# A decoder layer of self attention, cross attention and a quantised feed-forward on one core: orders rewritten step by step, grouped loads and stores, half of one mask moved from TensorE to VectorE

## The chip, the cores and the metric

The kernel runs on one core of a Trainium2 chip. The metric is device time in microseconds (us) of one execution, from the first to the last instruction of the program. Lower is better. The inputs are in the device's memory (HBM) before the time starts. How the host lays them out beforehand is not in the time.

## The reference

For each of B = 32 batches of S = 128 rows and D = 128 columns, three residual blocks follow one another, each on a layer-normalised x.

```python
x = x + self_attn(layernorm(x))        # 16 heads of 8, relative sinusoidal bias, no mask
x = x + cross_attn(layernorm(x), ctx)  # 16 heads of 8, keys and values from ctx, mask of padded keys
x = x + ffn(layernorm(x))              # w_down(silu(gate) * up), 128 -> 512 -> 128,
                                       # weights ternary, activations rounded to 8 bits
# attention: softmax(q @ k.T * scale + bias), masked scores set to -1e9, then @ v, then @ w_out
# ffn input and hidden rows: x * 127 / max|x|, rounded, each with its own scale
```

The batches are independent. Within a batch everything is a chain.

## The kernel before, in words

**Pipeline over batches.** One step of the program handles many batches, each at another stage. In the names S is self attention, X cross attention, F the feed-forward, and a lag is how many steps behind the newest batch a stage is: projections of S at lag 0, its scores for the maxima (scores A) at 2, its scores for the exponentials (scores B) and attention at 3, the same for X at 4, 5 and 6, its output and the first feed-forward half at 7, the second half at 8. So in a full step all engines work on nine batches. Steps 0 to 9 and 30 to 39 are written out. The twenty between are a loop on each engine with four steps in its body, and addresses and waited counts come from registers there.

**Order.** The five queues (TensorE = PE, VectorE = DVE, ScalarE = ACT, GpSimd = POOL, and SyncE = SP, which issues all DMAs) each run a fixed list of operations per step, `step(st)`, written by hand. Semaphores alone tie them together.

**Attention.** q and k are split into three bf16 parts each (`qk_parts`), written to a scratch in HBM (`parts_out`) and read back (`stack_in`) into `stack_q` and `stack_k`, so that one bf16 matmul with 72 (X) or 120 (S) rows gives a score to float32 accuracy. The 16 heads go in four chunks c = 0..3 of four heads, 512 columns, one bank. Scores A (L1059) go to `bank_a[c % 2]`; DVE takes the negative row maxima (`row_max`, L826), POOL splits them in two bf16 parts, PE transposes them (L1154, 32 columns), ACT copies them out, and SP stores them as two more rows of `stack_q` (`max_in`, L327). Scores B (L1092) then come out transposed and with the maximum subtracted in `bank_b[c % 2]`, and ACT takes the exponential (L533) into `probs`, which S and X share. `attend` (L1117) multiplies a chunk by the values in four column tiles of 32.

**Mask.** X alone has one. POOL makes `mask_bias` (0 or -1e30, bf16), and PE adds it to each chunk of scores A and scores B by one matmul of 512 columns with the identity:

```python
masked = a == "X"
if masked:
    pe.matmul(bank[:, :], ident_bf[:], mask_bias[:, p, :].unsqueeze(1).to_broadcast([S, HC, S]),
              start=True, stop=False)
```

**The rest.** `ctx` is loaded batch by batch (L337), transposed by PE (L1178) and copied by ACT (`ctxT_out`). The mask is loaded batch by batch (L347) and the result stored batch by batch (L356). x is loaded in three pieces, the last of 24 batches (1.5 MB) at step 2. `keep_warm` (L1026) puts four idle matmuls ahead of scores B of the first four batches. `normalise("S")` (L743) writes `xn_S`, `normalise("X")` `xn_X`; `residual` is L855; `o_transposed` is L1138; `h_gate` L894. POOL's `rest` is L432, `part3` L440.

## Time and profile before

| | |
|---|---|
| Median of 3 runs | 514.36 us (513.71 to 518.05) |
| Profiled execution, first to last instruction | 513.4 us |
| PE busy | 454.1 us, 88% |
| DVE busy | 398.0 us, 78% |
| ACT busy | 372.9 us, 73% |
| POOL busy | 254.6 us, 50% |
| DMA | 62.48 MB, mean 122 GB/s |
| Chain that ended last | PE 78% of the span |

The profiled execution took 513.4 us by its span, which is its own time too; no other time of it is given. Busy time of an engine is the union of its instructions; the weight loads of PE are counted apart. The shares are means over three stretches: a start of about 100 us in which the pipeline fills, some 300 us of full steps, and an end in which it empties. The term "turn" below means the time from one full step to the next.

### The profile page before, as it was taken

The numbers are of one execution on the slowest core, as the hardware profiler recorded it, in microseconds if no ns is written. First come the engines' busy times: TensorE is split into PE (matmuls) and PEld (weight loads), VectorE is DVE, ScalarE is ACT, GpSimd is POOL, SyncE is SP. The second block draws the span as 40 slices with busy tenths as digits, with TensorE's granted clock in tenths as the row PEclk, the third lists the DMA queues.
The fourth block names the chain that finished last, engine by engine and source line by source line (L and its number), as shares of the span: only waits on it lengthen the run. The fifth ranks groups of instructions, "written<-read, shape, count | busy, mean of one in ns | idle before, by whom it ended". The sixth has DMA issues, their size and how long they took to land.

```text
span 513.4 us, 18365 instructions
## 1 busy us (share of the span) xinstructions
PE 454.1 (88%) x5596; PEld 328.0 (64%) x5596; DVE 398.0 (78%) x1154; ACT 372.9 (73%) x993; POOL 254.6 (50%) x691
## 2 busy tenths in 40 slices
PE   2246889999999999999999999999999999997762
PEld 1224556777777777777777777777777777764440
DVE  5722446799888889888888988889888888877553
ACT  0222556788888888888888888888888887775451
POOL 4221445655565555555566655555556654434110
PEclk9999789999999999999999999999999999999785
DMA  6264255555455545454445555544454555223000
GB/s 186 77 192 107 72 143 142 140 142 141 134 134 144 141 122 145 139 135 131 122 138 135 135 128 135 137 135 122 133 137 137 137 137 136 79 86 92 23 7 10
DMA packets 82191, 62.48 MB, mean 122 GB/s; under 512 B 57634, under 2 KB 71714, under 8 KB 82146
## 3 DMA queue, kind: packets, MB, share of 16 engines
q1 hardware_dynamic: 82146, 61.92, 44.4%
q8 instruction: 23, 0.38, 0.3%
q14 instruction: 22, 0.18, 0.1%
HBM read 46.47 MB, written 14.88 MB: 119 GB/s over the span
## 4 chain that ended last, share of the span: by engine, by line
PE 78%; DVE 5%; DMA 4%; issue 4%; SPq 3%; ACT 3%; POOL 1%; DVEq 0%; POOLq 0%; ACTq 0%
PE bank L1117 14%; PE bank L1092 12%; PE bank L1059 11%; PE bank L1088 6%; PE bank L1055 6%; PE bank L1264 4%; PE bank L1210 3%; PE bank L1138 2%; PE bank L1237 2%; PE bank L1175 2%; PE bank L1154 2%; PE bank L1295 2%; PE bank L1303 2%; PE bank L1224 2%; PE bank L1196 2%
## 5 line engine op out<-in xcount | busy, mean ns | idle before, releaser
L533 ACT ACTIVATE probs<-bank 128x512 f32<-128x512 f32 x256 | 145.5, 597 | 32.0 <-PE bank L1092 31.7
L826 DVE TENSOR_REDUCE neg_max_S<-bank 128x4 f32<-128x512 f32 x128 | 87.1, 685 | 34.3 <-PE bank L1059 34.2
L826 DVE TENSOR_REDUCE neg_max_X<-bank 128x4 f32<-128x512 f32 x128 | 84.2, 676 | 8.9 <-PE bank L1059 5.7
L1059 PE MATMUL bank<-stack_k_S,stack_q_S 120*128 120x128 bf16 x512 | 46.9, 227 | 12.9 <-DMA stack_k_S<-scratch_S 12.4
L432 POOL TENSOR_TENSOR qk_rest_X<-qk_X,qk_parts_X 128x256 f32<-128x256 f32 x32 | 21.4, 670 | 70.8 <-ACT qk_parts_X L536 70.8
L1092 PE MATMUL bank<-stack_q_S,stack_k_S 122*128 122x128 bf16 x512 | 52.5, 229 | 4.5 <-DMA stack_q_S<-neg_maxT_S 4.5
L1117 PE MATMUL bank<-probs,v_aug_S 128*32 128x128 f32 x1024 | 55.5, 291 | 0.0
L1055 PE MATMUL bank<-mask_bias,ident_bf 128*128 128x512 bf16 x128 | 49.4, 386 | 3.6 <-issue 2.3
L1092 PEld LDWEIGHTS bank<-stack_q_X,stack_k_X 74*128 74x128 bf16 x512 | 40.6, 99 | 16.4 <-issue 1.6
L1092 PE MATMUL bank<-stack_q_X,stack_k_X 74*128 74x128 bf16 x512 | 50.8, 222 | 0.0
L1088 PE MATMUL bank<-ident_bf,mask_bias 128*128 128x512 bf16 x128 | 50.3, 393 | 0.0
L1059 PE MATMUL bank<-stack_k_X,stack_q_X 72*128 72x128 bf16 x512 | 50.1, 220 | 0.0
L1059 PEld LDWEIGHTS bank<-stack_k_X,stack_q_X 72*128 72x128 bf16 x512 | 39.9, 98 | 16.0 <-issue 0.6
L1059 PEld LDWEIGHTS bank<-stack_k_S,stack_q_S 120*128 120x128 bf16 x512 | 36.8, 101 | 15.3 <-issue 14.0
L1092 PEld LDWEIGHTS bank<-stack_q_S,stack_k_S 122*128 122x128 bf16 x512 | 32.4, 101 | 21.2 <-issue 7.8
L855 DVE TENSOR_TENSOR x_all<-bank,x_all 128x128 f32 (+1 forms) x64 | 18.6, 291 | 25.7 <-PE bank L1264 24.3
L536 ACT ACTIVATE o_raw<-bank 128x256 f32<-128x256 f32 x64 | 24.8, 388 | 16.7 <-PE bank L1117 16.7
L1117 PE MATMUL bank<-probs,v_aug_X 128*32 128x128 f32 x1024 | 34.6, 276 | 0.0
L440 POOL TENSOR_TENSOR qk_parts_S<-qk_rest_S,qk_parts_S 128x256 bf16<-128x256 f32 x32 | 21.6, 675 | 21.0 <-ACT qk_parts_S L536 21.0
L609 ACT ACTIVATE hT<-bank,minus_round 128x512 bf16<-128x512 f16 x32 | 22.0, 686 | 12.4 <-PE bank L1295 12.4
L1117 PEld LDWEIGHTS bank<-probs,v_aug_S 128*32 128x32 f32 x1024 | 20.6, 109 | 14.8 <-issue 1.2
L1117 PEld LDWEIGHTS bank<-probs,v_aug_X 128*32 128x32 f32 x1024 | 26.0, 109 | 4.8 <-ACT probs L533 1.3
(159 smaller groups left out, 1159.1 us busy)
## 6 DMA issues: line engine op xcount, KB each, us to landing
stack_q_S<-scratch_S SPq DMA_DIRECT2D x32, 288.0 KB
stack_k_S<-scratch_S SPq DMA_DIRECT2D x96, 96.0 KB
stack_q_X<-scratch_X SPq DMA_DIRECT2D x32, 288.0 KB
stack_k_X<-scratch_X SPq DMA_DIRECT2D x96, 96.0 KB
scratch_S<-qk_parts_S SPq DMA_DIRECT2D x32, 192.0 KB, 2.3
scratch_X<-qk_parts_X SPq DMA_DIRECT2D x32, 192.0 KB, 2.3
ctx_in<-ctx SPq DMA_DIRECT2D x32, 64.0 KB, 2.7
mask_in<-mask SPq DMA_DIRECT2D x32, 64.0 KB, 1.8
```

The lines of the kernel that those rows point to most:

```text
L432: pool.tensor_tensor(qk_rest[a][:], qk[a][:], qk_parts[a][:, :, 0, :], ALU.subtract)\
L440: pool.tensor_tensor(qk_parts[a][:, :, 2, :], qk_rest[a][:], qk_parts[a][:, :, 1, :], ALU.subtract).then_inc(sems["part3_" + a], 1)
L533: act.activation(probs[:, c, :], bank_b[c % 2][:, :], ACT.Exp).then_inc(sems["exp_" + a], 1)
L536: return act.activation(out_ap, in_ap, ACT.Copy)
L609: act.activation(hT[:].rearrange("p c s -> p (c s)"), bank_t[:, 0:256].bitcast(F16), ACT.Identity, bias=minus_round16[:, 0:1]).then_inc(se ...
L826: dve.tensor_reduce(neg_max[a][:, first_head(c):first_head(c) + 2 * HC - 1:2], bank_a[c % 2][:, :].rearrange("i (h j) -> i h j", h=HC), AX ...
L1055: pe.matmul(bank[:, :], ident_bf[:], mask_bias[:, p, :].unsqueeze(1).to_broadcast([S, HC, S]), start=True, stop=False)
L1059: last = pe.matmul(bank[:, part_of_bank(hh)], stack_q[a][rows, p, head(c, hh)], stack_k[a][rows, p, head(c, hh)], start=not masked, stop=n ...
L1088: pe.matmul(bank[:, :], mask_bias[:, p, :], ident_bf[:].unsqueeze(1).to_broadcast([S, HC, S]), start=True, stop=False)
L1092: last = pe.matmul(bank[:, part_of_bank(hh)], stack_k[a][rows, p, head(c, hh)], stack_q[a][rows, p, head(c, hh)], start=not masked, stop=n ...
L1117: last = pe.matmul(bank_o[32 * hh:32 * hh + 32, half * S:(half + 1) * S], v, probs[:, c, part_of_bank(hh)], start=u == 0, stop=u == 1, ski ...
L1264: pe.matmul(quarter(bank_s, 2), oT[a][:], w_o[a][:], start=True, stop=True)\
```

## The change

It keeps the pipeline of batches and all arithmetic except where said, and does the following.

- **Steps.** All 42 steps are written out; there is no loop and no register. Each operation takes the step and its own lag. Lags differ per engine by one where its list starts at another place of the step. On PE the operations are told which operations used their bank before (`*users`), and `after` waits for the first of these that exists.
- **Orders.** All five lists are new. On PE the four `attend("S")` stand together, as do the four of X.
- **Mask.** `BIASED = (0, 2)`: in chunks 0 and 2 of X's scores A, PE adds no mask. `row_max` on DVE adds it and takes the maximum head by head with `tensor_tensor_reduce`, instead of one `tensor_reduce` of four heads. Scores B keep the mask on PE.
- **Context.** The host hands `ctx` over transposed. PE's transpose and ACT's copy of it are gone. It and the mask are loaded for four batches at once (`group_load`), the results of the first 28 batches stored by four.
- **Buffers.** `probs` and `o_raw` are one each for S and X, values have four copies, the transposed `xn_X` goes to `bank_o`, and `neg_max_parts` is 128 wide with zeros, so that its transpose uses all 128 columns.
- q, k and v of a batch are projected together (`project_qkv`).

```diff
+STEPS = [(t, t) for t in range(-1, B + 9)]
+GROUP, GROUP_LAG = 4, 2
+BIASED = (0, 2)
...
-        probs = sb("probs", [S, CH, HC * S])
-        o_raw = sb("o_raw", [128, 2, S])
+        probs = {a: sb(f"probs_{a}", [S, CH, HC * S]) for a in "SX"}
+        o_raw = {a: sb(f"o_raw_{a}", [128, 2, S]) for a in "SX"}
+        biased = sb("biased", [S, CH, HC, S], BF16)
...
+            def group_load(st):
+
+                n = st.of("X", GROUP_LAG)
+                if n is None or n % GROUP:
+                    return
+                batches = slice(n, n + GROUP)
+                sp.dma_start(ctxT[:, batches, :], ctx[batches].rearrange("b d s -> d b s"))\
+                    .then_inc(sems[f"ctx_loaded{n // GROUP % 2}"], 16)
+                sp.dma_start(mask_in[:, batches, :], mask[batches].rearrange("b s t -> s b t"))\
+                    .then_inc(sems[f"mask_loaded{n // GROUP % 2}"], 16)
...
             def step(st):
-                if st.base == 2:
+                if st.of("S", 2) == 0:
                     load_x(2)
-                max_in("X", st.seq(B_X))
-                ctx_load(st.seq(CTX_T - 1))
-                stack_in("S", st.seq(FRONT_S + 1))
-                store(st.seq(FFN2))
-                parts_out("X", st.seq(FRONT_X))
-                max_in("S", st.seq(A_S))
-                mask_load(st.seq(A_X - 1))
-                parts_out("S", st.seq(FRONT_S))
-                stack_in("X", st.seq(FRONT_X))
...
+                group_load(st)
+                parts_out("S", st, 0)
+                stack_in("X", st, 4)
+                max_in("X", st, 5)
+                stack_in("S", st, 0)
+                parts_out("X", st, 3)
+                store(st, 7)
+                max_in("S", st, 1)
...
+                if a == "X" and c in BIASED:
+                    if c == BIASED[0]:
+                        dve.wait_ge(sems["mask_bias"], done(b))
+                        if b:
+                            dve.wait_ge(sems["max_X"], done(b - 1, CH))
+                    for hh in range(HC):
+                        head = first_head(c) + 2 * hh
+                        last = dve.tensor_tensor_reduce(biased[:, c, hh, :], quarter(bank_a[c % 2], hh), mask_bias[:, b % 2, :],
+                                                        -1.0, -2.0 * BIG, ALU.add, ALU.min,
+                                                        neg_max[a][:, head:head + 1])
+                    last.then_inc(sems["max_" + a], 1)
+                    return
...
+                masked = a == "X" and c not in BIASED
```

**PE, the part of a full step that holds the attention of S.** Before, with one `attend` of four matmuls at a time (`v_aug_S`), L1237 the transpose of X's output, L1224 and L1225 X's projections, L1264 its output projection:

```order
L1117 MATMUL bank<-probs,v_aug_S 32x128 x4
L1092 MATMUL bank<-stack_q_S,stack_k_S 128x128 x4
L1117 MATMUL bank<-probs,v_aug_S 32x128 x4
L1237 MATMUL bank<-ident,o_norm_X 128x128
L1224 MATMUL bank<-xnT_X,w_cross_sb 128x128
L1225 MATMUL bank<-ctxT,w_cross_sb 128x128
L1117 MATMUL bank<-probs,v_aug_S 32x128 x4
L1264 MATMUL bank<-w_out_x_sb,oT_X 128x128
L1036 REGISTER_ALU
L1059 MATMUL bank<-stack_k_S,stack_q_S 128x128 x4
L1117 MATMUL bank<-probs,v_aug_S 32x128 x4
```

And the same part after the change, where L1049 is scores B, L1029 scores A, L1065 `attend`, L1110 to L1112 the three projections, L1138 the output projection:

```order
L1049 MATMUL bank<-stack_q_S,stack_k_S 128x128 x4
L1110 MATMUL bank<-xnT_X,w_cross_sb 128x128
L1111 MATMUL bank<-ctxT,w_cross_sb 128x128
L1112 MATMUL bank<-w_cross_sb,ctxT 128x128
L1138 MATMUL bank<-w_out_x_sb,oT_X 128x128
L1029 MATMUL bank<-stack_k_S,stack_q_S 128x128 x4
L1065 MATMUL bank<-probs_S,v_aug_S 32x128 x16
L1161 MATMUL bank<-ident_h,h_q 128x128 x4
```

The four attentions of S, which stood apart between work on the whole array, are one block of sixteen.

**DVE, around the maxima of X, chunks 1 to 3.** Before:

```order
L743 TENSOR_SCALAR xn_S<-x_all,mv_S,rstd_S 128x128
L886 TENSOR_SCALAR y_q<-xn_F,y_inv 128x128
L822 REGISTER_ALU
L826 TENSOR_REDUCE neg_max_X<-bank 128x4
L822 REGISTER_ALU
```

```order
L797 TENSOR_REDUCE neg_max_X<-bank 128x4
L862 TENSOR_SCALAR y_q<-xn_F,y_inv 128x128
L703 TENSOR_SCALAR xn_S<-x_all,mv_S,rstd_S 128x128
L792 ISA biased,neg_max_X<-bank,mask_bias 128x128
L792 ISA neg_max_X 128x1
```

The normalisation of S has moved behind the rounding of y and the maxima of chunk 1, and the pair of L792 rows stands four times in a row for chunk 2 and four times for chunk 0, eight pairs in a step for two reductions.

**SP, from the second batch's scratch at the start of the program.** Before, with the third piece of x, one context, the stacks of batch 1 and the maxima of batch 0:

```order
L288 DMA scratch_S<-qk_parts_S 128x6x128
L233 DMA x_all<-x 128x24x128
L337 DMA ctx_in<-ctx 128x128
L306 DMA stack_q_S<-scratch_S 72x1x2048
L311 DMA stack_k_S<-scratch_S 24x1x2048 x3
L327 DMA stack_q_S<-neg_maxT_S 2x16x128
```

After:

```order
L271 DMA scratch_S<-qk_parts_S 128x6x128
L283 DMA stack_q_S<-scratch_S 72x1x2048
L288 DMA stack_k_S<-scratch_S 24x1x2048 x3
L300 DMA stack_q_S<-neg_maxT_S 2x16x128
L222 DMA x_all<-x 128x24x128
L309 DMA ctxT<-ctx 128x4x128
L311 DMA mask_in<-mask 128x4x128
L271 DMA scratch_S<-qk_parts_S 128x6x128
L283 DMA stack_q_S<-scratch_S 72x1x2048
L288 DMA stack_k_S<-scratch_S 24x1x2048 x3
L300 DMA stack_q_S<-neg_maxT_S 2x16x128
```

The large load of x has moved behind the stacks of batch 1 and the maxima of batch 0, now together with four contexts and masks, and ahead of the scratch, stacks and maxima of the next batch.

## Rows read from the trace of the kernel before

**Rows 1.** The page's chain of work that ended last, by engine.

```profile
PE 78%; DVE 5%; DMA 4%; issue 4%; SPq 3%; ACT 3%; POOL 1%; DVEq 0%; POOLq 0%; ACTq 0%
```

**Rows 2.** A window of full steps: length, busy us (instructions) per engine, PEclk, DMA, GB/s.

```profile
200.00:300.00 100.00, 99.47 (x1299) 73.39 (x1296) 88.52 (x261) 86.49 (x233) 57.43 (x155) 1.00 0.49 134
```

**Rows 3.** Timeline of ACT, one instruction per step: start us, duration us.

```profile
103.27 0.71 ACT L656 ACTIVATE tanh_g<-bank,gate_half 128x512 f32<-128x512 f32 x1
116.30 0.71 ACT L656 ACTIVATE tanh_g<-bank,gate_half 128x512 f32<-128x512 f32 x1
...
249.86 0.71 ACT L656 ACTIVATE tanh_g<-bank,gate_half 128x512 f32<-128x512 f32 x1
...
356.94 0.71 ACT L656 ACTIVATE tanh_g<-bank,gate_half 128x512 f32<-128x512 f32 x1
...
409.81 0.71 ACT L656 ACTIVATE tanh_g<-bank,gate_half 128x512 f32<-128x512 f32 x1
```

**Rows 4.** The chain in order of time, one full step: start us, us, what.

```profile
250.04 1.01 PE bank L1117 x32
251.05 0.33 PE bank L1092 x4
251.53 0.33 PE bank L1092 x4
251.87 0.22 PE bank L1138 x2
...
252.54 0.23 PE bank L1092 x4
...
253.30 0.36 PE bank L1117 x8
...
257.27 0.22 PE bank L1055
...
263.29 1.01 PE bank L1117 x32
```

**Rows 5.** Timeline of DVE in a full step; in brackets idle before, and for whom.

```profile
276.69 0.29 DVE L855 TENSOR_TENSOR x_all<-bank,x_all 128x128 f32 x1
276.90 0.28 DVE L724 BATCH_NORM_STATS2 stats_S<-x_all 128x6 f32 x1
...
281.17 0.14 DVE L938 TENSOR_TENSOR h_scale<-h_inv,h_unit 128x1 f32<-128x1 f32 x1
281.24 0.68 DVE L826 TENSOR_REDUCE neg_max_S<-bank 128x4 f32<-128x512 f32 x1
282.37 0.29 DVE L855 TENSOR_TENSOR x_all<-bank,x_all 128x128 f32 x1 [0.45 <-PE bank L1264]
282.59 0.69 DVE L826 TENSOR_REDUCE neg_max_S<-bank 128x4 f32<-128x512 f32 x1
283.20 0.28 DVE L724 BATCH_NORM_STATS2 stats_F<-x_all 128x6 f32 x1
...
286.84 0.79 DVE L743 TENSOR_SCALAR xn_S<-x_all,mv_S,rstd_S 128x128 f32 x1
```

**Rows 6.** Timeline of POOL at the same time.

```profile
286.87 0.67 POOL L432 TENSOR_TENSOR qk_rest_S<-qk_S,qk_parts_S 128x256 f32<-128x256 f32 x1 [0.24 <-ACT qk_parts_S L536]
```

**Rows 7.** Groups by line and shape: busy us, mean ns, idle before.

```profile
L826 DVE TENSOR_REDUCE neg_max_X<-bank 128x4 f32<-128x512 f32 x128 | 84.2, 676 | 8.9 <-PE bank L1059 5.7
L743 DVE TENSOR_SCALAR xn_S<-x_all,mv_S,rstd_S 128x128 f32 x20 | 15.4, 772 | 0.0
L536 ACT ACTIVATE ctxT<-bank 128x128 f32<-128x128 f32 x32 | 8.8, 276 | 0.0
L743 DVE TENSOR_SCALAR xn_X<-x_all,mv_X,rstd_X 128x128 f32 x20 | 6.9, 346 | 3.1 <-POOL rstd_X L416 2.3
```

**Rows 8.** Timeline of SP's DMA issues at the start of the program.

```profile
29.45 0.90 SPq L233 DMA_DIRECT2D x_all<-x  x1
30.40 5.66 SPq L337 DMA_DIRECT2D ctx_in<-ctx  x1
...
39.22 0.70 SPq L327 DMA_DIRECT2D stack_q_S<-neg_maxT_S  x1
```

**Rows 9.** Timeline of PE, first scores B of batch 0.

```profile
42.73 1.03 PE L1092 MATMUL bank<-stack_q_S,stack_k_S 122*128 122x128 bf16 x8 [4.50 <-DMA stack_q_S<-neg_maxT_S]
```

More of the change, by code:

```diff
@@ L211, in first_head, with done, loaded, in_group @@
             return H // 2 * (c // 2) + c % 2
[L213 to L225 removed]
+        def done(b, per=1, upto=None):
+            return b * per + (per if upto is None else upto)
+        def loaded(b, per):
+            return (b // 2 + 1) * per
+        def in_group(b):
+            return (b // GROUP // 2 + 1) * 16
+        def after(eng, st, *users):
+            for name, lag, *signal in users:
+                stage = name[-1] if name[-2:] in ("_S", "_X") else "F"
+                b = st.of(stage, lag)
+                if b is not None:
+                    eng.wait_ge(sems[name], done(b, CH, signal[0]) if signal else done(b))
+                    return
+        def run(step):
+            for s, x in STEPS:
+                step(Step(s, x))
         block = es.enter_context(nc.Block())
@@ L995, in _ @@
+                ln_moments("S", st, -1)
+                gated(st, 8)
+                attend_sums("X", st, 7)
+                normalise("X", st, 4)
+                attend_norm("X", st, 7)
+                h_max(st, 8)
+            run(step)
         @block.tensor
@@ new lines, in scores_a @@
+                if masked:
+                    pe.wait_ge(sems["mask_bias"], done(b))
+                    pe.matmul(bank[:, :], ident_bf[:], mask_bias[:, b % 2, :].unsqueeze(1).to_broadcast([S, HC, S]),
+                              start=True, stop=False)
+                for hh in range(HC):
+                    last = pe.matmul(bank[:, part_of_bank(hh)], stack_q[a][rows, b % 2, head(c, hh)],
+                                     stack_k[a][rows, b % 2, head(c, hh)], start=not masked,
+                                     stop=not masked or hh == HC - 1)
@@ new lines, in scores_a, with scores_b @@
+                last.then_inc(sems["score_a_" + a], 1)
+            def scores_b(a, st, lag, c, *users):
+                b = st.of(a, lag)
+                if b is None:
+                    return
+                bank, rows = bank_b[c % 2], slice(0, A_ROWS[a] + M_ROWS)
+                after(pe, st, *users)
+                if c == 0 and a == "S" and b < WARM_BATCHES:
+                    keep_warm(bank)
+                if c == 0:
+                    pe.wait_ge(sems[f"max_in_{a}{b % 2}"], loaded(b, 16))
@@ L1094, in scores_b, with attend @@
+                    last = pe.matmul(bank[:, part_of_bank(hh)], stack_k[a][rows, b % 2, head(c, hh)],
+                                     stack_q[a][rows, b % 2, head(c, hh)], start=not masked,
                                      stop=not masked or hh == HC - 1)
                 last.then_inc(sems["score_b_" + a], 1)
-            def attend(a, st, b, c):
-                if not b:
+            def attend(a, st, lag, c, *users):
+                b = st.of(a, lag)
+                if b is None:
```

1233 lines of the change are left out of this document (543 added, 690 removed).

## The prediction

> **What bounds the kernel now.** I read first the chain that ended last: PE holds 78% of it and nothing else more than 5% [rows 1]. Then the window of full steps: in 100 us PE is busy 99.5, DVE 88.5, ACT 86.5, POOL 57.4, at full clock and half-used DMA engines [rows 2]. So in full steps PE is the bound and two engines run close behind it; the reader should see that 11 us of each 100 is all that a cheaper PE can win before DVE is the bound. Third, one instruction per step on ACT gives the turn. From 103.27 to 409.81 us lie 23 turns, 13.33 us each; the first of them, outside the loop, took 13.03, eight in the loop took 107.08, 13.39 each [rows 3]. So 23 full turns are 306.5 of the 513.4 us; the start takes 103 and the end another 103. The profiled span, 513.4, lies 1.0 below the median of 514.36; I work on the span and add 1.0 at the end.
>
> **PE, part by part.** In the chain one full step runs from 250.04 to 263.29 [rows 4].
>
> - Loop: written out, a turn is 13.03 instead of 13.33 on average: -0.30. The price of it, more instructions to fetch, shows nowhere in the written-out steps of before.
> - Two mask matmuls of 512 columns go, 0.22 each on the chain [rows 4]: -0.44.
> - The context's transpose: two transposes of 128 columns took 0.22 (L1138) [rows 4], one is 0.11: -0.11. ACT loses a copy of 0.28 [rows 7].
> - The attentions of S: apart, four matmuls (counted as 8) cost 0.36, so four times 1.44; X's sixteen in a block cost 1.01 [rows 4]. In a block: -0.43.
> - What follows a matmul that uses 32 columns costs more: scores B took 0.33 behind the attention of X and behind the transposed maxima (251.05 and 251.53) and 0.23 elsewhere (252.54) [rows 4]. Three places behind S's attentions and two behind the transposed maxima go, at 0.10 each: -0.5, between 0.2 and 0.9 as the gap of 0.15 ahead of 251.53 is also theirs or is not.
>
> Sum: 13.33 - 1.8 = 11.55 us per turn of PE work (11.2 to 11.9). If PE stayed the bound, that would be 41 us off 23 turns.
>
> **DVE, part by part.** Its busy time is 88.5% of 13.33 = 11.8 us per turn [rows 2].
>
> - Out: two reductions of 512 columns, 0.68 each [rows 7]: -1.35.
> - In: eight times an addition with maximum over 128 columns, with the accumulator read behind it (two instructions by the build), which the trace of before does not show. I bound a pair from both sides. What counts is the distance between starts, not the duration: the addition of the same shape with one operand in a bank lasts 0.29 but the next one starts 0.21 later; the reduction lasts 0.69 and its follower starts 0.61 later; an instruction of one column lasts 0.14 and its follower starts 0.07 later [rows 5]. So 0.28 a pair at the low end. At the high end nothing overlaps, since the read needs the finished sum: 0.29 + 0.15 = 0.44. I take 0.31, near the low end, as all three rows show the overlap: +2.5 (2.25 to 3.5).
> - `xn_S` lasts 772 ns in the loop, the same operation of X 346 [rows 7]; it runs from 286.84 to 287.63, beside POOL's subtraction from 286.87 to 287.54, and ends just after it [rows 5, 6]. In the new order it stands elsewhere; whether it meets POOL again I cannot see: between -0.43 and 0, I take -0.2.
> - The register instructions go; they are not in the busy time.
>
> Sum: 11.8 - 1.35 + 2.5 - 0.2 = 12.75 us (12.3 to 13.9). That is more than PE's 11.55: **DVE becomes the bound**, and of PE's 1.8 us most has nowhere to go. DVE now waits 0.45 us for X's output projection (L1264) and elsewhere in each turn [rows 5]; with PE 1.2 us ahead of it such waits should nearly vanish. I leave 0.05. A turn of **12.8 us**.
>
> [...]
>
> **ACT and POOL.** ACT's 86.5% is 11.5 us, less the copy of 0.28: 11.25, still below. POOL has 7.7 of 13.3. The chain around a step from S's projection over ACT, POOL, ACT (parts, values) to `gate_up`, `tanh` and `gate` has little slack in the new order. It is covered as long as DVE has its row maxima to do; were that cover gone, I would expect a wait of some 0.3 us at `h_gate`.
>
> **SP and the DMAs.** The maxima of X are stored after `stack_in("X")` as before. PE now wants them nearer to their transpose: between L1088 of X and the first scores B of X stand about 3.8 us of PE work by the prices of rows 4, before about 6 (from 251.5 to 257.5) [rows 4]. The path of copy, issue and landing took 3.5 us at the start, where one was issued at 39.22 and its reader began at 42.73 [rows 8, 9]. That is close, but PE has 1.2 us to spare. Grouped loads and stores save SP issues only, and SP is nowhere in the chain of full steps: 0.
>
> **Start.** Before, the load of 24 batches of x went out at 29.45, the next issue behind it took 5.66 us, and the maxima of batch 0, issued at 39.22, reached PE at 42.73 [rows 8, 9]. Now these maxima and the stacks of batch 1 go first, and I expect those scores 3 us earlier. But then x with four contexts and masks, a third more bytes (2.0 MB), stands ahead of the scratch, stacks and maxima of the next batch, which PE wants 12 us later. The gain is given back there: 0, plus or minus 3.
>
> **The sum.** 23 full turns: 23 x (12.8 - 13.33) = -12.2. Start and end have about nine turns with attention but no feed-forward or no new batch, in which DVE has less to do and PE's saving counts in part; I take 0.5 each, -4.5 (0 to -9). The last turns, pure latency of one batch, stay. 513.4 - 12.2 - 4.5 = 496.7, and with 1.0 for the median **497.5 us**. With the turn between 12.5 and 13.0 it is 490 to 503.
>
> **The rivals.**
>
> - *PE stays the bound or the pair is cheap (0.25), and `xn_S` is free of POOL.* DVE is then at 12.05, PE at 11.55, the turn about 12.2: -26, and -6 outside: 482. For it: the overlap in rows 5. Against it: no row has an accumulator read.
> - *Waits take half the gain.* DVE is the bound and PE must wait for it in every bank pair; PE's fixed order then makes ACT or DVE idle for 0.4 us in each turn, at `h_gate` or at the maxima of X that come late. Turn 13.2: -3, and -3 outside: 508. For it: 0.45 us and more of such waits now, and three engines above 11 us.
> - *Slower: the accumulator read waits for its instruction's end.* One mechanism on DVE at L792: 8 x 0.44 = 3.5, the turn 13.85, +12 over 23 turns, -4 outside: 522. It decides from a pair of 0.37 on, where DVE reaches 13.25, the turn of today.
> - *The change does not do what it says:* PE's cheaper step is not seen as the 32-column switches stay, and DVE and PE both end near 13.2: the loop's 0.3 is cancelled, 512.
>
> **How the numbers follow.** Forecast 0.50, cheap pair 0.13, waits 0.17, slower 0.13, no effect 0.07. Less than 1%, 5 us, cannot be told from no change in this kernel. Faster by over 1% (under 509): 0.50 + 0.13 and two thirds of the waits, 0.75. Slower by over 1% (over 519.5): 0.10. Same: 0.15. For the range I leave out part of the cheap case and the slower one: 483 to 514.
>
> **What would show it.** In the profile after, DVE should be busy 95% or more in full steps and PE near 90%; the chain should name DVE lines, L792 first, instead of 78% PE. Sixteen attentions of S should take 1.0 us. The eight pairs should take 2.5 us from first to last start of their blocks; at 3.5 the forecast is wrong and the kernel slower. `xn_S` should be near 350 or near 770 ns. The first scores B should start near 40 us and the start as a whole should be no shorter. Wrong would make it: a price of the pair far from 0.31, waits of DVE for PE or ACT of more than 0.5 us per turn, or straight-line code that makes an engine wait for its instructions.

## The result, and the profile after

The changed kernel took 505.03 us (median of 4 runs, 497.83 to 509.43), the kernel before in the same session 516.20 (4 runs, 513.71 to 520.06): ratio 0.9685, 95% interval 0.960 to 0.977, faster. The ratio is taken over the fast executions alone, which are 497.83 and 502.48 of the changed kernel (median 500.2) and all four of before; by the two medians it would be 0.978. The forecast was 497.5 in a range of 483 to 514. The profiled execution is the fastest of the four: 497.83 us, span 496.0, against 513.4 before.

The page after has these lines on the engines and on the chain.

```profile
PE 412.5 (83%) x5500; PEld 316.3 (64%) x5500; DVE 402.9 (81%) x1602; ACT 364.7 (74%) x961; POOL 251.3 (51%) x693
issue 30%; POOL 24%; DMA 14%; PE 13%; SPq 8%; DVE 5%; ACT 4%; POOLq 0%; ACTq 0%; DVEq 0%
DMA stack_k_X<-scratch_X 7%; SPq L288 3%; POOL qk_rest_X L400 3%; POOL mask_bias L437 3%; POOL qk_rest_S L400 3%; POOL qk_parts_X L409 3%; DMA scratch_S<-qk_parts_S 2%; PE bank L1029 2%; POOL x_all L390 2%; PE bank L1049 2%; DMA scratch_X<-
```

Of the 78% of [rows 1] PE keeps 13% of the chain. DVE, which the forecast named, has 5%. POOL has 24%, in many lines of at most 3%, and 30% is time in which an engine waited for nothing that the profile shows. What heads the lines that can be named is a transfer, the load of X's stacks. The windows say why: the first is the one of [rows 2], the other two are two neighbouring turns.

```profile
200.00:300.00 100.00, 96.01 (x1368) 75.62 (x1356) 95.05 (x392) 89.39 (x241) 60.81 (x168) 1.00 0.54 145
233.26:245.53 12.27, 12.02 (x175) 9.48 (x179) 11.92 (x50) 11.17 (x30) 7.58 (x22) 1.00 0.48 133
245.53:258.64 13.11, 12.14 (x175) 9.53 (x178) 11.84 (x50) 11.36 (x30) 7.91 (x22) 1.00 0.66 184
```

PE and DVE are each busy 95% or more. In the second turn PE is busy 0.12 us more than in the first and DVE 0.08 less; it is 0.84 us longer because both wait. ACT's one instruction per step gives all turns, as in [rows 3].

```profile
105.00 0.69 ACT L613 ACTIVATE tanh_g<-bank,gate_half 128x512 f32<-128x512 f32 x1
...
245.53 0.69 ACT L613 ACTIVATE tanh_g<-bank,gate_half 128x512 f32<-128x512 f32 x1
258.64 0.69 ACT L613 ACTIVATE tanh_g<-bank,gate_half 128x512 f32<-128x512 f32 x1
...
395.39 0.69 ACT L613 ACTIVATE tanh_g<-bank,gate_half 128x512 f32<-128x512 f32 x1
```

There are two kinds of turn: a **quiet turn** of 12.27 us, and between such ones a **long turn** of 13.0 to 13.8; of the 23 turns from 105.00 to 395.39, seven are long. The mean is 290.39 / 23 = 12.63. PE's timeline in the long turn above answers to [rows 4].

```profile
250.15 1.08 PE L1065 MATMUL bank<-probs_S,v_aug_S 128*32 128x128 f32 x32
251.20 0.40 PE L1161 MATMUL bank<-ident_h,h_q 128*128 128x128 f16 x4
...
252.75 0.38 PE L1029 MATMUL bank<-stack_k_X,stack_q_X 72*128 72x128 bf16 x4 [0.81 <-DMA stack_k_X<-scratch_X]
```

S's sixteen attentions now stand in one block, 1.05 us from start to next start. PE then stands still for X's stack, 0.81 us. DVE at the same time, as in [rows 5]:

```profile
253.17 0.29 DVE L792 CUSTOM_DVE_ANT_0 biased<-bank,mask_bias 128x128 bf16<-128x128 f32 x1 [0.59 <-PE bank L1029]
253.38 0.08 DVE L792 DVE_READ_ACCUMULATOR2_ANT neg_max_X<- 128x1 f32 x1
253.38 0.29 DVE L792 CUSTOM_DVE_ANT_0 biased<-bank,mask_bias 128x128 bf16<-128x128 f32 x1
253.59 0.08 DVE L792 DVE_READ_ACCUMULATOR2_ANT neg_max_X<- 128x1 f32 x1
...
256.38 0.49 DVE L862 TENSOR_SCALAR y_q<-xn_F,y_inv 128x128 f16<-128x128 f32 x1
256.80 0.33 DVE L703 TENSOR_SCALAR xn_S<-x_all,mv_S,rstd_S 128x128 f32<-128x128 f32 x1
```

From one pair to the next is 0.21 us, and the accumulator read starts together with the next addition (both at 253.38): it adds nothing to the 0.21 us from the addition of `residual` at 276.69 to its follower [rows 5]. Over the program the two L792 groups below have 256 records each, 32 batches by eight heads, so one `tensor_tensor_reduce` stands in the trace as an addition and a read. Within a block of four, additions start 0.20 to 0.22 us apart, 192 times, and each time the read has the start of the next addition. In this turn `xn_S` is free of POOL, and `y_q` has its place beside POOL's addition, which ran from 256.34 to 256.80. In the quiet turn before it both meet POOL, with 0.51 us for `y_q` and 0.49 for `xn_S`; in the kernel before they took 0.289 and 0.772 in the mean. The groups over the whole program, as in [rows 7]:

```profile
L792 DVE CUSTOM_DVE_ANT_0 biased<-bank,mask_bias 128x128 bf16<-128x128 f32 x256 | 58.6, 283 | 13.4 <-PE bank L1029 13.3
L792 DVE DVE_READ_ACCUMULATOR2_ANT neg_max_X<- 128x1 f32 x256 | 20.6, 81 | 0.0
L862 DVE TENSOR_SCALAR y_q<-xn_F,y_inv 128x128 f16<-128x128 f32 x32 | 14.1, 440 | 0.1
L703 DVE TENSOR_SCALAR xn_S<-x_all,mv_S,rstd_S 128x128 f32<-128x128 f32 x32 | 14.0, 437 | 5.9 <-POOL rstd_S L383 5.9
```

The quiet turn has a chain over three engines that the trace of before did not show as a wait: `y_q` on DVE, its transpose on PE, the copy `yT` on ACT, S's output projection on PE (L1138), and the residual on DVE.

```profile
243.16 0.51 DVE L862 TENSOR_SCALAR y_q<-xn_F,y_inv 128x128 f16<-128x128 f32 x1
243.73 0.23 PE L1130 MATMUL bank<-ident_h,y_q 128*128 128x128 f16 x1
244.10 0.36 ACT L584 ACTIVATE yT<-bank,minus_round 128x128 bf16<-128x128 f16 x1
244.60 0.46 PE L1138 MATMUL bank<-w_out_s_sb,oT_S 128*128 128x128 f32 x2 [0.17 <-ACT yT L584]
245.10 0.29 DVE L827 TENSOR_TENSOR x_all<-bank,x_all 128x128 f32<-128x128 f32 x1 [0.17 <-PE bank L1138]
```

From 105 to 402 us PE waits for `yT` 16 times, 2.8 us in all, and DVE for that projection 23 times, 4.4 us; PE's waits of the kernel before, from 103 to 410 us, have no such line.

SP's issues and PE at the start answer to [rows 8, 9].

```profile
38.03 0.70 SPq L300 DMA_DIRECT2D stack_q_S<-neg_maxT_S  x1
39.28 0.85 SPq L222 DMA_DIRECT2D x_all<-x  x1
```

```profile
40.06 0.62 PE L1049 MATMUL bank<-stack_q_S,stack_k_S 122*128 122x128 bf16 x8 [2.01 <-DMA stack_q_S<-neg_maxT_S]
...
57.83 1.03 PE L1049 MATMUL bank<-stack_q_S,stack_k_S 122*128 122x128 bf16 x8 [2.47 <-DMA stack_q_S<-neg_maxT_S]
```

The first scores B start at 40.06 instead of 42.73; those of the next batch, at 57.83, came at 55.44 before.

Where the stack waits come from is seen in SP's issues around that turn, before in the first fence and after in the second, which begins with a quiet turn's.

```profile
277.12 2.01 SPq L311 DMA_DIRECT2D stack_k_X<-scratch_X  x3
```

```profile
233.84 2.03 SPq L288 DMA_DIRECT2D stack_k_X<-scratch_X  x3
...
244.16 0.41 SPq L309 DMA_DIRECT2D ctxT<-ctx  x1
244.63 0.50 SPq L311 DMA_DIRECT2D mask_in<-mask  x1
245.23 0.45 SPq L271 DMA_DIRECT2D scratch_S<-qk_parts_S  x1
...
246.62 2.03 SPq L288 DMA_DIRECT2D stack_k_X<-scratch_X  x3
```

Before, the last of X's stacks was issued by 279.1 and its scores A began at 283.78: 4.7 us. After, it is issued by 248.65, and PE would have begun at 251.94: 3.3 us, and in this turn 0.5 MB of contexts and masks stand ahead of it in the queue. In the quiet turn the last is issued by 235.87 and its scores A begin at 239.51 without a wait: 3.6 us are just enough there. In the long turn the stack is there 4.1 us after its issue. PE waits for X's stack six times from 105 to 402 us, 6.6 us in all, and the seventh long turn has 0.7 us at the same place, where the view names a maximum of DVE. Two of the six (1.20 us at 124.87, 1.45 at 176.94) have no grouped load ahead of them; why those stacks came late is not traced.

### The profile page after: what moved, and what is told of

It reads as the page before. It is cut to its first block, busy times and chain, and to the rows that moved or that the text cites. A ratio compares the mean times of both kernels' runs of the same rounds, so it can differ in the third digit from the quotient of the medians.

```text
span 496.0 us, 17508 instructions
## 1 busy us (share of the span) xinstructions
PE 412.5 (83%) x5500; PEld 316.3 (64%) x5500; DVE 402.9 (81%) x1602; ACT 364.7 (74%) x961; POOL 251.3 (51%) x693
## 4 chain that ended last, share of the span: by engine, by line
issue 30%; POOL 24%; DMA 14%; PE 13%; SPq 8%; DVE 5%; ACT 4%; POOLq 0%; ACTq 0%; DVEq 0%
DMA stack_k_X<-scratch_X 7%; SPq L288 3%; POOL qk_rest_X L400 3%; POOL mask_bias L437 3%; POOL qk_rest_S L400 3%; POOL qk_parts_X L409 3%; DMA scratch_S<-qk_parts_S 2%; PE bank L1029 2%; POOL x_all L390 2%; PE bank L1049 2%; DMA scratch_X<-qk_parts_X 2%; POOL rstd_F L383 2%; POOL rstd_S L383 2%; SPq L283 2%; PE bank L1110 1%
## 5 line engine op out<-in xcount | busy, mean ns | idle before, releaser
L506 ACT ACTIVATE probs_S<-bank 128x512 f32<-128x512 f32 x128 | 73.0, 599 | 10.0 <-PE bank L1049 10.0
L506 ACT ACTIVATE probs_X<-bank 128x512 f32<-128x512 f32 x128 | 72.4, 595 | 10.4 <-PE bank L1049 10.4
L792 DVE CUSTOM_DVE_ANT_0 biased<-bank,mask_bias 128x128 bf16<-128x128 f32 x256 | 58.6, 283 | 13.4 <-PE bank L1029 13.3
L1029 PE MATMUL bank<-stack_k_X,stack_q_X 72*128 72x128 bf16 x512 | 50.0, 220 | 12.6 <-DMA stack_k_X<-scratch_X 9.6
L1029 PE MATMUL bank<-stack_k_S,stack_q_S 120*128 120x128 bf16 x512 | 46.1, 224 | 10.7 <-DMA stack_k_S<-scratch_S 10.2
L1029 PEld LDWEIGHTS bank<-stack_k_X,stack_q_X 72*128 72x128 bf16 x512 | 37.5, 98 | 23.7 <-DVE neg_max_S L797 11.1
L1049 PEld LDWEIGHTS bank<-stack_q_X,stack_k_X 74*128 74x128 bf16 x512 | 40.6, 99 | 16.2 <-issue 1.6
L1049 PE MATMUL bank<-stack_q_X,stack_k_X 74*128 74x128 bf16 x512 | 50.7, 222 | 0.0
L1049 PE MATMUL bank<-stack_q_S,stack_k_S 122*128 122x128 bf16 x512 | 45.8, 224 | 4.8 <-DMA stack_q_S<-neg_maxT_S 4.8
L1029 PEld LDWEIGHTS bank<-stack_k_S,stack_q_S 120*128 120x128 bf16 x512 | 36.1, 100 | 13.0 <-issue 10.6
L797 DVE TENSOR_REDUCE neg_max_X<-bank 128x4 f32<-128x512 f32 x64 | 43.3, 677 | 0.0
L1049 PEld LDWEIGHTS bank<-stack_q_S,stack_k_S 122*128 122x128 bf16 x512 | 34.5, 101 | 13.5 <-DMA stack_q_S<-neg_maxT_S 6.7
L1065 PE MATMUL bank<-probs_S,v_aug_S 128*32 128x128 f32 x1024 | 35.4, 280 | 0.0
L1065 PE MATMUL bank<-probs_X,v_aug_X 128*32 128x128 f32 x1024 | 34.6, 276 | 0.0
L1065 PEld LDWEIGHTS bank<-probs_X,v_aug_X 128*32 128x32 f32 x1024 | 26.0, 109 | 13.3 <-ACT probs_X L506 13.1
L400 POOL TENSOR_TENSOR qk_rest_S<-qk_S,qk_parts_S 128x256 f32<-128x256 f32 x32 | 21.4, 668 | 24.7 <-ACT qk_parts_S L509 24.6
L827 DVE TENSOR_TENSOR x_all<-bank,x_all 128x128 f32<-128x128 f32 x64 | 18.7, 291 | 17.6 <-PE bank L1138 16.8
L623 ACT ACTIVATE h_q<-h,round,h_scale 128x512 f16<-128x512 f32 x32 | 26.1, 814 | 5.0 <-DVE h_scale L924 5.0
```

The costliest lines, as they stand in the source:

```text
L400: pool.tensor_tensor(qk_rest[a][:], qk[a][:], qk_parts[a][:, :, 0, :], ALU.subtract)\
L506: act.activation(probs[a][:, c, :], bank_b[c % 2][:, :], ACT.Exp).then_inc(sems["exp_" + a], 1)
L623: act.activation(h_q[:], h[:], ACT.Identity, bias=round16[:, 0:1], scale=h_scale[:, 0:1])\
L792: last = dve.tensor_tensor_reduce(biased[:, c, hh, :], quarter(bank_a[c % 2], hh), mask_bias[:, b % 2, :], -1.0, -2.0 * BIG, ALU.add, ALU.min,
L797: dve.tensor_reduce(neg_max[a][:, first_head(c):first_head(c) + 2 * HC - 1:2], bank_a[c % 2][:, :].rearrange("i (h j) -> i h j", h=HC), AX ...
L827: dve.tensor_tensor(x_all[:, b, :], quarter(bank_s, 2), x_all[:, b, :], ALU.add)\
```

## The experiments

Each is the changed kernel with one edit, unless it says the kernel before. Ratios are to the kernel before, run between them on the same chip.

### Loads one batch at a time

```diff
-GROUP, GROUP_LAG = 4, 2
+GROUP, GROUP_LAG = 1, 2
```

> The changed kernel with contexts and masks loaded and results stored batch by batch (GROUP = 1 instead of 4), all else as in the change. In the changed kernel three turns of four last 12.26 us and the fourth 12.9 to 13.5; in the fourth, scores A of X wait for the stacks of X to land. Theory 1 (the burst of eight contexts and masks stands ahead of the stacks in the DMA queues): all turns become about 12.3, the DMA waits at scores A of X vanish in full steps, and the time falls by 5 to 9 us against the changed kernel (497.8 to 509.4), to 490 to 500. Theory 2 (the fourth turn is long for another reason, for instance the stored results or fetching of instructions): the pattern of four stays with GROUP = 1, or every turn grows by a little, and the time stays within 3 us.

Measured: 507.77 us, ratio 0.983 (0.975 to 0.991). The quiet turn stays 12.27, but eleven of 23 turns are long and the mean is 13.01 against 12.63. PE's waits from 105 to 402 us:

```profile
PE bank L1029 <- DMA stack_k_X<-scratch_X: 12.9, 13, 2.2
```

In the changed kernel that line reads 6.6 us, 6 times, 1.5 at most. So the pattern of four is gone, and neither theory holds as written: with a small load ahead of the stack in every turn, the waits for it come more often. Grouping moves these loads out of three of four turns, from in front of a stack that has little margin. I had put it at 0. The two profiled executions differ by 0.4 us a turn, but what grouping is worth in the time is not shown: 3.1 of the 8.8 us between the 23 turns are two falls of the clock (below), the profile here is of the slowest of four executions and the changed kernel's of the fastest, and the intervals of the two ratios overlap.

### All masks on PE, and all on DVE

```diff
-BIASED = (0, 2)
+BIASED = ()            # second kernel: (0, 1, 2, 3)
```

> The changed kernel with the whole mask on PE (BIASED empty): four pairs of reductions per turn come back as on the kernel before, in the new order. Theory 1 (VectorE is the bound at 12.27 us, the pairs cost 8 x 0.21 = 1.7 us there, two reductions 1.2 us, and PE has some 0.5 us or more to spare): a quiet turn of 11.8 to 12.1 us, the kernel 4 to 10 us faster than the changed one. Theory 2 (the moved mask is what makes the change fast, since PE is still as good as the bound): turn 12.7, 10 to 12 us slower than the changed one.

> The changed kernel with the whole mask of X's scores A on VectorE (BIASED = all four chunks). Theory 1 (VectorE is the bound): 16 pairs at 0.21 = 3.4 us instead of 1.7 + 1.2, so +0.5 us per turn, a quiet turn of 12.8 us and 12 to 15 us more than the changed kernel. Theory 2 (PE as good as the bound): turn 11.9 to 12.3, the same or 5 to 9 us faster.

Measured: all on PE 502.75, ratio 0.975 (0.967 to 0.983); all on DVE 504.20, ratio 0.981 (0.972 to 0.991). Both intervals overlap that of the changed kernel (0.960 to 0.977); the quiet turns tell them apart. The first row is a quiet turn with all masks on PE, the second with all on DVE.

```profile
284.38:296.77 12.39, 12.14 (x176) 9.70 (x181) 11.27 (x36) 11.35 (x30) 7.56 (x22) 1.00 0.51 134
```

```profile
230.39:242.91 12.52, 11.69 (x172) 9.28 (x175) 12.18 (x66) 11.19 (x31) 7.60 (x22) 1.00 0.47 131
```

With no pair on DVE the turn is 12.39 and PE's; with sixteen it is 12.52 and DVE's; with eight it is 12.27. Both theories of either run missed: each named one engine as the bound, and the turn grew in both directions. A mask matmul costs 0.22 us [rows 4], a reduction 0.61 [rows 5] and a pair 0.21 from start to start. If the end turns were all work, the changed kernel would have 12.39 - 2 x 0.22 = 11.95 us of it on PE and 12.52 - 8 x 0.21 + 2 x 0.61 = 12.06 on DVE. These are upper bounds, since both engines also wait in these turns; from the busy times, 12.14 and 12.18, the same sums give 11.70 and 11.72. The turn of 12.27 lies above all of them. **Of the three splits tried, two of four has the shortest quiet turn, and the whole move of the masks is worth 0.12 us a turn**, about 3 us of the time, which the medians can't show. PE's 0.44 has nowhere to go, as DVE is as full.

### The last load of x two steps later

```diff
-                if st.of("S", 2) == 0:
+                if st.of("S", 4) == 0:
                     load_x(2)
```

> The changed kernel with the third piece of x (24 batches, 1.5 MB) loaded at step 4 instead of step 2; the groups of contexts and masks stay at step 2. Theory 1 (that load stands ahead of the scratch, stacks and maxima of batches 1 and 2 and costs the start 5 to 8 us): the second batch's scores B begin near 51 to 53 us instead of 57.8 and the first tanh comes 3 to 6 us before 105.0; a wait of the same kind may appear later in the start and take back a part. Theory 2 (the start is bound by the chain of one batch per step, not by the load): the first tanh stays within 1 us of 105.

Measured: 499.96, ratio 0.972 (0.963 to 0.980), first tanh at 103.33 instead of 105.00, quiet turn 12.28, seven long turns in 23 as in the changed kernel. The second batch's scores B start at 50.05 instead of 57.83, so that load was in their way as theory 1 says, but 1.7 us is left of it at the first tanh, between the two theories. In the time it is nothing that can be told from the changed kernel.

### The kernel before, written out

```diff
-LOOP_FROM, LOOP_TO = 10, 30
+LOOP_FROM, LOOP_TO = 10, 10
```

> The kernel before with all 40 steps written out and no loop, nothing else. Theory 1 (the loop costs 0.3 us per turn, as the turns of before outside the loop last 13.03 to 13.2 and those inside 13.39): all full turns about 13.0 to 13.2, 4 to 7 us faster than before. Theory 2 (fetching of straight-line instructions costs as much as the loop): no change, within 2 us.

Measured: 507.38, ratio 0.987 (0.983 to 0.990). A turn:

```profile
216.22:229.25 13.03, 12.97 (x175) 9.78 (x174) 11.83 (x36) 11.44 (x33) 7.77 (x23) 1.00 0.55 139
```

It goes on at 13.02, with 13.96 once and two of about 13.35; 23 turns take 301.2 us instead of 306.5, as theory 1 says. So **the loop cost 5.4 us there and about 7 in the time**, some two fifths of the whole gain (0.0135 of 0.0315, each with its interval).

### S's attentions apart in the new order

```diff
+                attend("S", st, 3, 0, ("xnT_X", 4), ("o_raw_X", 7), ("o_raw_S", 4))
                 project_qkv("X", st, 4, ("h", 8), ("v_S", 1), ("v_X", 5))
+                attend("S", st, 3, 1)
                 project_out("X", st, 7)
+                attend("S", st, 3, 2)
                 scores_a("S", st, 2, 2, ("max_S", 2, 1), ("max_X", 6, 3), ("max_X", 6, 1), ("max_S", 3, 3))
-                attend("S", st, 3, 0, ("xnT_X", 4), ("o_raw_X", 7), ("o_raw_S", 4))
-                attend("S", st, 3, 1)
-                attend("S", st, 3, 2)
                 attend("S", st, 3, 3)
```

> The changed kernel with the four attentions of S taken apart again on PE (0 ahead of X's projections, 1 ahead of X's output projection, 2 behind it, 3 behind the third chunk of scores A). PE's work grows by 0.4 us for the attentions and up to 0.3 for what follows them. Theory 1 (PE is within 0.5 us of the bound in the changed kernel): quiet turns of 12.5 to 12.9 us, 6 to 15 us slower than the changed kernel. Theory 2 (VectorE alone is the bound and PE has a whole us to spare, as the prediction has it): quiet turns stay at 12.3, time as the changed kernel's.

Measured: 521.34, ratio 1.012 (1.009 to 1.015): slower than the kernel before, with all else of the change in place. The turn and PE in it:

```profile
226.21:239.49 13.28, 12.91 (x174) 9.36 (x178) 11.92 (x50) 11.29 (x31) 7.58 (x22) 1.00 0.44 121
```

```profile
230.84 0.43 PE L1065 MATMUL bank<-probs_S,v_aug_S 128*32 128x128 f32 x8
231.20 0.49 PE L1138 MATMUL bank<-w_out_x_sb,oT_X 128*128 128x128 f32 x2
231.62 0.43 PE L1065 MATMUL bank<-probs_S,v_aug_S 128*32 128x128 f32 x8
```

Four times 0.36 from start to start against 1.05 in a block; and the output projection between two attentions takes 0.42, which in the changed kernel, between others, takes 0.22 (212.81 to 213.03). DVE's work is the same 11.92. **The block is worth 1.0 us in every quiet turn**, more than anything else tested, and more than theory 1 said: 0.39 of it are the attentions, the rest what stands around them in this order. One thing more shows here. With the turn at 13.28 the margin of X's stack grows again, to 4.1 us and more from issue to use in most turns, and of the 23 turns two are long instead of seven; PE's waits for that stack fall from 6.6 to 2.8 us. That fits the margin as the cause of most long turns.

### Narrow and wide transposes

The kernel before, with the halves of the maxima 128 columns wide (zeros beyond the 32 in use).

```diff
-        neg_max_parts = {a: sb(f"neg_max_parts_{a}", [S, M_ROWS, H], BF16) for a in "SX"}
+        neg_max_parts = {a: sb(f"neg_max_parts_{a}", [S, 128], BF16) for a in "SX"}
...
-                pe.transpose(half_words.bitcast(BF16)[0:M_ROWS * H, :],
-                             neg_max_parts[a][:].rearrange("s m h -> s (m h)"), ident_bf[:])\
+                pe.transpose(half_words.bitcast(BF16), neg_max_parts[a][:], ident_bf[:])\
```

> The kernel before, with the transposed halves of the maxima 128 columns wide instead of 32, and nothing else changed. Theory 1 (what follows a 32-column transpose pays for the switch on TensorE): scores B behind the transpose take 0.23 instead of 0.33 us each, the turn falls by 0.2 to 0.3 us, the time by 5 to 8 us, ratio 0.985 to 0.990. Theory 2 (the wide transpose costs as much as the switch that it saves, and the 0.33 us is only how the end is modelled): the turn stays at 13.2 to 13.3 and the ratio at 0.998 to 1.002.

Measured: 513.75 us (12 runs), ratio 0.996 (0.993 to 1.000). PE saves what theory 1 says, the turn does not: PE's share in the first row, the chain of the same kernel in the rows behind.

```profile
220.70:233.97 13.27, 13.11 (x176) 9.75 (x174) 11.92 (x36) 11.61 (x33) 7.83 (x22) 1.00 0.52 135
```

```profile
249.25 0.06 PE bank L1155
...
255.79 0.18 DVE mv_F L736
...
256.39 0.58 POOL rstd_F L417
...
257.00 0.36 DVE xn_F L744
```

PE is busy 13.11 instead of 13.27, and the chain now leaves it for the normalisation ahead of the feed-forward, statistics on DVE, root on POOL, and back. Neither theory holds as written. It is the transpose itself whose follower starts sooner, after 0.06 us instead of 0.16, at each of two places, and in the old order another chain, as long to within 0.16 us, takes PE's place.

### X's stacks first in SP's list

The second kernel has single loads as well.

```diff
-                group_load(st)
-                parts_out("S", st, 0)
                 stack_in("X", st, 4)
+                parts_out("S", st, 0)
                 max_in("X", st, 5)
                 stack_in("S", st, 0)
+                group_load(st)
```

> The changed kernel with SP's list altered: the read of X's stacks comes first in a step, ahead of the store of S's parts, so that it no longer waits for POOL's last part of S, and the grouped loads stand behind the read of S's stacks instead of ahead of everything. In the changed kernel the last of the reads for X is issued some 2.8 us before scores A of X want it, and about ten of 23 full turns last 0.7 to 1.5 us longer with a wait for it. Theory 1 (that landing is the cause of the long turns and of most of the spread between runs): issue 0.7 us earlier and no load ahead of it, most long turns vanish, 4 to 9 us faster than the changed kernel, runs of it closer together. Theory 2 (the long turns come from the volume of transfers wherever they stand): about as many long turns remain.

> As e8_stack_first, and contexts, masks and results batch by batch (GROUP = 1). With the loads one by one but ahead of the stacks (e1_single) the kernel had about twice as many long turns as the changed one. Theory 1 (what counts is what stands ahead of X's stacks in the queue, not whether loads are grouped): now no load stands there in either kernel, both have few long turns and come out within 3 us of each other, and this one has the smaller worst turn. Theory 2 (single loads are worse by themselves, by more issues and more small transfers): this one stays 5 us or more slower than e8_stack_first.

Measured: 550.64, ratio 1.069 (1.066 to 1.073), and 549.42, ratio 1.067 (1.062 to 1.072). Both theories of the first missed. The second is within 3 us of the first, as its theory 1 says, but not for the reason given there: most turns are long in both. SP's own waits in 200 to 300 us, with grouped loads:

```profile
SPq L283 <- DMA scratch_S<-qk_parts_S: 18.2, 7, 3.3
SPq L283 <- DMA scratch_X<-qk_parts_X: 15.1, 7, 3.6
```

A stack's load is held until the parts have landed in memory, 2.2 to 2.6 us in the mean, and what stands behind it in SP's list is issued after it. In the changed kernel the issues between `parts_out` and `stack_in` cover that (1.2 and 0.2 us left in the same stretch); here SP stands still 33 us in 100. The margin of the stacks can't be bought at the head of SP's list.

### The grouped load in SP's gap, and two more moves

In the changed kernel SP waits 2.7 us in each turn for `qk_parts_X` (21.8 us in 100). The first kernel puts the grouped load there; the second also makes X's third part earlier on POOL; the third also has the late load of x.

```diff
-                group_load(st)
                 parts_out("S", st, 0)
                 stack_in("X", st, 4)
                 max_in("X", st, 5)
                 stack_in("S", st, 0)
+                group_load(st)
...
                 max_hi("S", st, 2)
-                variance("S", st, -1)
                 max_lo("S", st, 2)
+                part3("X", st, 4)
+                variance("S", st, -1)
                 inverse_std("S", st, -1)
-                part3("X", st, 4)
```

> The grouped loads of ctx and mask stand behind the loads of S's stacks in SyncE's list instead of at the head of a step, so they are issued in the stretch of 2.7 us in which SyncE waits for qk_parts_X, and nothing that a score waits for is queued behind them but the parts of X. Theory 1, the grouped load ahead of the X stacks makes every fourth turn long (13.1 to 13.8 us instead of 12.27, 5 to 6 of the ten long turns): those turns become 12.3, PE's waits on stack_k_X halve, and the time falls by 4 to 7 us against the changed kernel (ratio to the kernel before near 0.955 to 0.962). Theory 2, the X stacks land late of themselves, since they are issued only 6 us before they are wanted: the long turns stay, at other places, and the ratio stays at 0.967 to 0.972.

> As the run above, and on GpSimd the third part of X's q and k (L409) is made before the variance and the rsqrt of S instead of behind them, 0.8 us earlier in each turn; SyncE waits for just that before it stores the parts of X. Theory 2 (the margin of the X stacks is near zero in every turn): the stacks of X land 0.8 us earlier, the long turns that are left go, every turn of the middle is 12.3, and the ratio falls to 0.950 to 0.958. Theory 1 (only the grouped load): no more than 1 us from the run above. A third way: rstd_S, now 0.7 us later, delays xn_S on VectorE and the quiet turn grows by 0.1 to 0.3 us, which gives 3 to 9 us back.

> As the run above, and the last load of x (1.6 MB) is issued two steps later. If the moves are worth what they are worth alone, the first tanh comes 1.5 us earlier than in the changed kernel and the time is 1 to 3 us under the run above; if the late load of x then meets the loads of the stacks of the first turns, these turns are longer and it is the same within 1 us.

Measured: 501.59, ratio 0.968 (0.963 to 0.973); 502.33, ratio 0.974 (0.970 to 0.979); 502.43, ratio 0.970 (0.965 to 0.976). None is to be told from the changed kernel's 0.9685. (In the profiled execution of the first the granted clock was 0.89 from 60 to 105 us, against 0.99 in the changed kernel's; that is ahead of the turns told of here.) PE's waits from 105 to 402 us, of the first and then of the second:

```profile
PE bank L1029 <- DMA stack_k_X<-scratch_X: 4.9, 8, 1.5
PE bank L1049 <- DMA stack_q_S<-neg_maxT_S: 4.8, 5, 1.6
```

```profile
PE bank L1029 <- DMA stack_k_X<-scratch_X: 4.1, 5, 1.3
```

In the first, every fourth turn stays long (13.5 to 14.3). Half a megabyte in SP's gap now stands ahead of the parts of X and the maxima of S; PE waits for these maxima, a wait that the changed kernel does not have from 105 to 402 us, and still for X's stack (1.45 us at 215.67, its load issued 1.7 us nearer to its use than in a quiet turn). The wait has spread rather than gone. In the second, the first eight turns are all quiet, where the changed kernel had four long ones and the first kernel four of 12.6 to 13.9. That fits theory 2, by one execution of each. But a quiet turn is 12.41 instead of 12.27. The third way foreseen had the sign and the size of it and not the cause: DVE does not wait for `rstd_S`. `y_q` ends 0.08 us after POOL's subtraction in both kernels, and that has run for 0.10 us when `y_q` starts here, for 0.24 in the changed kernel: 0.65 us instead of 0.51. Four turns in 23 are over 12.6 instead of seven, mean 12.56 instead of 12.63: 1.4 us won in the turns, within the noise of the whole. With the late load of x as well, the first tanh is at 105.24, so the 1.5 us did not come, and the mean turn is 12.71. No version beats the changed kernel beyond what the runs can tell.

## Why the prediction came out as it did

The sign, the size in the profiled execution (span 496.0, forecast 496.7) and the range are right. The median is 7.5 us above the forecast. That the span comes within 1 us is in part luck: the full turns gave 3.9 us more than forecast and start and end 3.2 less, and in the turn itself a pair that was too dear stands against waits that were put at nothing. The quiet turn, 12.27, is that of the rival "cheap pair" (12.2); only the long turns bring the mean, 12.63, near the 12.8 of the forecast.

- **Full turns.** Forecast 23 x -0.53 = -12.2, measured 290.4 - 306.5 = -16.1. Quiet turns fell by 1.0 us; seven long turns gave 8.1 us back.
- **The pair on DVE**: 0.31 was mis-sized; it took 0.21, under my low bound of 0.28. I had added an instruction of one column behind the addition, but the read runs inside the overlap. Eight pairs are 1.7 us instead of 2.5, and DVE's sum becomes 12.75 - 0.8 = 11.95; it measured 11.92. This is the rival "cheap pair" for DVE. The sum is not quite of one kind: it takes out the two reductions at their duration, 0.68, where their starts are 0.61 apart, which is 0.13 us the other way.
- **PE's sum**, 11.55, was a little low: 11.70 by the busy time with all masks on PE, at most 11.95 by the turn. The loop (-0.24 in quiet turns, and the 0.5 at every fourth) and the block with its followers (0.73 forecast, 0.9 of PE's work measured) are as forecast or better, and the transposed maxima give 0.2 as forecast. What the changed kernel's quiet turn has above 11.7 is for the most part no work: ahead of S's output projection, scores A take 0.56 us from start to next start (244.04 to 244.60) instead of 0.22, because PE waits for `yT`. The rest, some 0.2 us, stays open.
- **DVE becomes the bound, PE 1.2 us ahead**: wrong. In a quiet turn PE is busy 12.02 us and DVE 11.92, and the turn is 0.25 longer than PE's; that much of the rival "waits take half the gain" is true, on the way from `y_q` over PE and ACT back to DVE. So PE had nothing to spare when a transfer was late.
- **SP and the DMAs: 0.** This is the step that failed. I looked at the maxima of X and called them covered by PE's slack; they make one wait, of 0.5 us. I did not look at X's stacks, whose margin in the order fell from 4.7 us to 3.6, and to 3.3 behind a grouped load. Their late landing is in all long turns but one the larger part of what these have above a quiet one, or all of it.
- **`xn_S`**: 437 ns in the mean instead of 772, and `y_q` 440 instead of 289, as POOL now stands beside both: together -0.18, so -0.2 was fair.
- **Start.** Scores B 2.7 us earlier, given back by the next batch's 2.4 us later; first tanh +1.7. Two kernels whose start has the order of before had it 2.2 us (wide transposes) and 4.4 us (written out) earlier than before, so this is within the scatter. Start and end together: -1.3 where -4.5 stood.
- **The slower rival** fell with the first row of pairs. If nothing overlapped, a pair would be 0.36 us even at this trace's own 283 and 81 ns; starts lie 0.21 apart. The 0.44 under this rival was an estimate: no run shows such a pair or the turn of 13.85, and with sixteen pairs (all masks on DVE) the quiet turn is 12.52.
- **The median above the profiled run.** The kernel's executions scatter by 12 us, those of before by 6. The traces show one way in which this can come about. With all masks on PE there is one turn of 16.41 us; these are PE's wait in it and two windows behind that.

```profile
251.45 0.38 PE L1026 MATMUL bank<-mask_bias,ident_bf 128*128 128x512 bf16 x1 [2.23 <-issue]
```

```profile
252.00:254.00 2.00, 2.00 (x16) 1.89 (x14) 1.58 (x4) 0.60 (x1) 0.50 (x1) 0.58 0.57 128
254.00:256.00 2.00, 2.00 (x14) 1.42 (x14) 0.32 (x3) 1.27 (x4) 0.47 (x1) 0.57 0.71 181
```

PE stood still for 2.2 us and then ran at a granted clock of 0.57 in the mean of these 4 us, 0.50 from 253 to 255, before it was back at 1.00 from 256 on. With all masks on DVE one turn is 15.94, behind a wait of 1.94 us for X's stack, and with single loads two are 16.03 and 15.48, behind stack waits of 2.21 and 1.65 us; the granted clock was 0.50 from 252 to 255 us in the first of these profiles, and from 127 to 129 and from 181 to 184 in the second. The turn of 16.41 is 4.0 us longer than a quiet one, 2.2 by the wait; the other 1.8 I put down to the clock, as 4 us at 0.57 instead of 1.00 lose 1.7 (an estimate). (This wait's releaser isn't shown; it stands where the changed kernel waits for X's stack.) The length of the wait alone does not decide: behind the waits of up to 1.5 us in the changed kernel's profile the clock stayed 1.00 (150 to 157 us, around the wait of 1.50), and so it did behind one of 2.12 us in the kernel with all three moves (1.00 from 265 to 270).

```profile
265.53 0.38 PE L1029 MATMUL bank<-stack_k_X,stack_q_X 72*128 72x128 bf16 x4 [2.12 <-DMA stack_k_X<-scratch_X]
```

That turn took 14.42 us, the wait and no more. That the changed kernel's 509 us execution had turns with a fallen clock is argued, not shown: only the fastest was profiled.

## What to carry to other kernels

When a change evens out two engines and makes the step shorter, list again the margin of every transfer that an engine waits for: here 1 us less per step turned a stack load with 4.7 us of margin into the wait that shows, 6.6 us from 105 to 402 us, and 1 us more brought these waits down to 2.8 us. Before moving a small load, ask what stands behind it in the queue at its new place. Keep matmuls of one shape together where the order lets you: the quiet turn was 12.27 us with S's attentions in one block and 13.28 with them apart, and these four moved lines outweighed all else that was tested.

## What the runs showed of the hardware beyond that

- In the changed kernel's trace the `tensor_tensor_reduce` of L792 (128 columns, one operand in a bank) starts every 0.21 us within a block of four (0.20 to 0.22, 192 times), with its accumulator read; the addition lasts 283 ns and the read 81 ns in the mean of 256 each, and the read starts at the same time as the next addition.
- `attend`'s matmuls, which use 32 columns: eight records between other work take 0.36 us to the next start (229.62 to 229.98 with S's attentions apart), 32 records in a block 1.05 (250.15 to 251.20 in the changed kernel), so 0.26 for eight. X's output projection takes 0.42 us between two such groups (231.20 to 231.62, attentions apart) and 0.22 between other work (212.81 to 213.03, changed kernel).
- A `tensor_scalar` of 128 columns on DVE that had a POOL operation beside it from its start (the first of these from 0.03 us on) ended 0.07 to 0.09 us after that operation, in four places: `xn_S` of before (0.79 us, POOL to 287.54), `y_q` and `xn_S` of the changed kernel's quiet turn (0.51 and 0.49, POOL to 243.59 and 244.01), `y_q` of its long turn (0.49, POOL to 256.80). An `xn_S` of the changed kernel that started 0.14 us ahead of POOL's operation (256.80 against 256.94) took 0.33.
- The changed kernel, 42 steps written out, fetched 45 + 45 packets of instructions, 1.11 MB in all, and the kernel before 23 + 22, 0.56 MB. In the quiet turn from 233.26 to 245.53 the waits listed for PE and DVE are one of 0.2 us for `yT` and one of 0.2 us for S's output projection, none for instructions.
